# Token routing scattered in two halves, zero fills moved into a later layer, chunk rows loaded ahead of stores, and contexts loaded earlier

## The chip, the core and the metric

The program runs on one core of one Trainium2 chip. The metric is device time in microseconds (us), from the start of the program to its end. Three timed runs of the kernel before took 1674.0, 1676.03 and 1676.31 us; the median is 1676.03 us. The profile comes from one more execution. Engines are named as in the profile: PE is TensorE (PEld its weight loads), DVE is VectorE, ACT is ScalarE, POOL is GpSimd and SP is SyncE, which here only issues transfers (DMAs).

## The reference, cut to what matters

Eight sequences of 112 tokens with 256 features pass through four layers. Each layer adds a gated cross attention and a gated feed-forward part:

```python
x = x + tanh(g_xattn[2]) * L2_xattn(layernorm(x), ctx, ctx, mask_BxSxS2)   # 16 heads, 375 keys, one mask per sequence
x = x + tanh(g_ffn[2])   * L2_ffn(layernorm(x))                            # two blocks, each attention + experts
# first block of L2_ffn: _token_moe
cw  = top-2 softmax weights of h @ gate_w + gate_b           # 8 experts, 2 for each token
out = sum over e of (gelu(h @ w1[e] + b1[e]) @ w2[e] + b2[e]) * cw[..., e]
```

The other parts are computed too, but the change touches only their neighbourhood: layer 1 has 16 experts whose tokens are chosen by capacity (its rows come back through memory) and a shared expert, and layer 2's feed-forward has a second block whose experts are chosen for a whole sequence.

## The kernel before, in words

Every engine has its instruction stream written out by hand, in the order of the code; semaphores tie them together. The eight sequences are taken as two groups (`it` = 0, 1, called the first and the second group here) of four sequences (lanes, `j`). SP issues nearly all loads in one stream, and waits in that stream for the moment at which a buffer is free.

Layer 2's cross attention ("l2x") needs for each lane a context (`arena<-in_ctxT`, 375 KB) and a mask (`arena<-in_mask`, 164 KB). SP waits for the end of layer 1's shared expert (`end["sh"]`) and then issues context and mask lane by lane. For the second group each context waits for that lane's last values of the first group. PE starts a group with `keys_ahead` (lanes 0 and 1 in the second group), then transposes, then keys and queries (L581); DVE first turns the four masks into numbers (L2213).

The token experts ("tok") work on chunks of 128 rows of one expert. All 1792 token-expert pairs get a slot in a table in memory, `token_rows`. Before, the slots of an expert begin where the chunks that the experts ahead of it use end, so a slot is known only when all pairs of both groups are counted: PE counts the picks (L1851), sums them over experts (L1855), and gives the slots (L1857 to L1859); DVE makes `token_slots` of them (L2396). POOL then scatters the rows, 16 indirect DMAs (L1272), waits until they have landed, reads the number of turns into a register, and loads the rows of the first two chunks (L1280). A turn is four chunks; here there are five turns. In a turn, for each chunk PE multiplies it by the expert's first matrix (16 products of two passes), transposes the rows of the chunk after the next (L1869), and multiplies a chunk's hidden values by the second matrix. POOL waits for the transposition of a chunk's rows, which frees their buffer, loads the rows of two chunks further, and stores finished outputs (`token_outputs`, L1291). SP loads each expert's weights, 2 MB, for the next turn when PE has finished that chunk. At the end POOL gathers the outputs by the same slots (L1300).

Rows of `token_rows` that no token fills, and part of `token_outputs`, must be zero: two DMAs early in the program fill them from one block of zeros. Lines 1074 to 1078 hold these fills, 1121 to 1127 the contexts and masks, 1266 to 1292 POOL's scatter and its loop.

Of the kernel before, what the change touches and what calls it, by code (L numbers as in the profile page):

```python
# [19 lines left out]
F32 = mybir.dt.float32  # L20
BF16 = mybir.dt.bfloat16
I32 = mybir.dt.int32
# [104 lines left out]
def flamingo(nc, A, out):  # L127
    ctx = ExitStack()
    with ctx:
# [54 lines left out]
        tok_ids = sb("chunk_experts", [1, MAX_TURNS * TOK_SLOTS + 1], I32)  # L184
        hmean = sb("h_mean", [P, 2, LANES, KC])
# [145 lines left out]
        idf = arena[0:1, 3 * LB + 2400:3 * LB + 2430]  # L331
        tok_hid = [arena[:, s * LB + 2048:s * LB + 2048 + 8 * P] for s in range(2)]
# [649 lines left out]
        at["n"] = 0  # L982
        xn_all = cut(arena, B * C)[0:T, :].rearrange("t (b c) -> t b c", b=B)
        sel = cut(arena, CAP * P)[0:T, :].rearrange("t (c g) -> t c g", c=CAP)
        selw = cut(arena, CAP * P)[0:T, :].rearrange("t (g c) -> t g c", c=CAP)
        expert_rows = arena[0:T, 0:2 * B * C].rearrange("s (b h f) -> s b h f", b=B, h=2)
        xnT_all = cut(arena, KC * B * T).rearrange("p (k b t) -> p k b t", k=KC, b=B)
        taken = cut(arena, KC * E1 * B * CAP).rearrange("p (k e n) -> p k e n", k=KC, e=E1)
        selT = cut(arena, B * 2 * T)[0:T, :].rearrange("s (b h t) -> s b h t", b=B, h=2)
        eo = cut(arena, E1 * C)[0:T, :].rearrange("s (e c) -> s e c", e=E1)  # L990
        hbuf = [cut(arena, 4 * T) for _ in range(2)]
# [9 lines left out]
        tok_rows = nc.dram_tensor("token_rows", ((MAX_TURNS * TOK_SLOTS + 2) * P, C), F32, kind="Internal").ap()  # L1001
        tok_outs = nc.dram_tensor("token_outputs", (MAX_TURNS * TOK_SLOTS * P, C), F32, kind="Internal").ap()
# [32 lines left out]
        def _(sp):  # L1035
# [32 lines left out]
            for dst, name in ((w_sg, "ws_g"), (w_su, "ws_u"), (w_sd, "ws_d"), (w_gate1, "l1_gate"),  # L1068
# [42 lines left out]
            for i in range(E1 // EX_SLOTS):  # L1111
                rows_of_turn(i)

# [78 lines left out]
        def _(g):  # L1192
# [74 lines left out]
            g.wait_ge(s_route, 8)  # L1267
            g.wait_ge(*p["normed"].at(0, f_norms(0)[NORM_B2], LANES - 1))
            for b in range(B):
                for k in range(TOP2):  # L1270
                    n = b * TOP2 + k
                    g.indirect_dma_start(tok_rows, bass.IndirectOffsetOnAxis(ap=tok_slot[:, n:n + 1], axis=0),  # L1272
                                         hrow[b % LANES][:, b // LANES, :], None).then_inc(s_scat, 16)
            g.wait_ge(s_scat, 16 * PAIRS)
            g.wait_ge(s_tid, 2)
# [3 lines left out]
            def chunk_rows(it, r):  # L1279
                g.dma_start(tok_x[r % 2], tok_rows[bass.ds((it * TOK_SLOTS + r) * P, P), :]).then_inc(s_xr[r % 2], 16)  # L1280

            for r in range(2):
                chunk_rows(0, r)
# [1401 lines left out]
```

## Time and profile before

| What | Value |
|---|---|
| timed runs, median (lowest to highest) | 1676.03 us (1674.0 to 1676.31) |
| profiled execution, its own time | 1660.98 us |
| its span | 1659.6 us |
| mean granted TensorE clock | 0.97 of full speed |
| PE busy / weight loads busy | 1539.6 us (93%) / 1272.0 us (77%) |
| DVE / ACT / POOL busy | 747.2 (45%) / 680.7 (41%) / 241.7 us (15%) |
| share of PE and of DMA in the chain that ended last | 70% and 5% |
| SP's queue | 97515 packets, 143.53 MB |

The profiled execution is 15.05 us shorter than the median of the timed ones; 1.4 us of it lie outside its span. The span runs through the stages one after the other: layer 0 until about 231 us, layer 1 until 488, layer 2's cross attention until 665, the first block of its feed-forward with the token experts until 970, the second block until 1229, and layer 3 to the end. Times in the views are us from the start of the span. In a row, "idle before" in brackets is how long the engine stood idle before the instructions, and what ended that.

### The profile page before, as it was taken

How to read it: one execution, taken by the hardware profiler on the slowest of the kernel's cores; microseconds unless marked ns; L12 is line 12 of the kernel's file. 1: busy time of each engine (PE TensorE's matmuls, PEld its weight loads, DVE VectorE, ACT ScalarE, POOL GpSimd, SP SyncE). 2: the span in 40 equal slices, each digit the busy share in tenths (PEclk: the TensorE clock that was granted, in tenths of full speed). 3: DMA queues.
4: the chain of work that ended last, by engine and by line, in shares of the span. 5: the costliest groups of instructions: out<-in, count | busy, mean ns of one | idle time of the engine just before them, and what ended most of it. 6: DMA issues, size and time to landing. Idle time of an engine off the chain costs nothing.

```text
span 1659.6 us, 32141 instructions
## 1 busy us (share of the span) xinstructions
PE 1539.6 (93%) x12101; PEld 1272.0 (77%) x12101; DVE 747.2 (45%) x2634; ACT 680.7 (41%) x2151; POOL 241.7 (15%) x379
## 2 busy tenths in 40 slices
PE   7999999799989999998699978999999999999986
PEld 5787887688977777775588866878987777777865
DVE  3535565411036666864011157771124443444466
ACT  2615433322117676754233326643334443344452
POOL 2022210000001121212311133156000000000000
PEclk9999999899999999998799999889999999999999
DMA  9500011359210100401789910337930001000000
GB/s 335 204 1 1 1 42 38 115 204 292 49 54 1 55 2 2 182 2 47 238 301 310 309 36 24 103 102 239 300 109 1 1 1 38 1 1 2 1 1 23
DMA packets 103253, 156.38 MB, mean 94 GB/s; under 512 B 12231, under 2 KB 80959, under 8 KB 102535
## 3 DMA queue, kind: packets, MB, share of 16 engines
q1 hardware_dynamic: 97515, 143.53, 26.2%
q0 software_dynamic: 3552, 9.18, 1.6%
q8 instruction: 86, 1.41, 0.4%
q10 hardware_dynamic: 2048, 1.84, 0.3%
q14 instruction: 52, 0.43, 0.1%
HBM read 147.31 MB, written 11.67 MB: 96 GB/s over the span
## 4 chain that ended last, share of the span: by engine, by line
PE 70%; ACT 7%; DMA 5%; DVE 5%; issue 3%; POOL 2%; POOLq 0%; ACTq 0%; DVEq 0%
PE psum L581 43%; PE psum L678 6%; PE psum L662 5%; PE psum L702 5%; PE psum L968 5%; ACT arena L889 4%; DMA arena<-token_rows 3%; DMA expert_out<-arena 1%; PE psum L537 1%; POOL token_rows L1272 1%; PE psum L955 1%; ACT arena L903 1%; PE psum L710 1%; PE psum L547 1%; DVE arena L801 1%
## 5 line engine op out<-in xcount | busy, mean ns | idle before, releaser
L889 ACT ACTIVATE arena<-arena,rowmin 112x375 f32<-112x375 f32 (+1 forms) x584 | 292.6, 507 | 180.4 <-DVE rowmin L801 180.3
L581 PE MATMUL psum<-arena,region 128*128 128x112 f32 (+2 forms) x1920 | 325.6, 327 | 5.2 <-DMA arena<-in_ctxT 2.6
L581 PEld LDWEIGHTS psum<-arena,region 128*128 128x128 f32 x1920 | 261.9, 197 | 66.1 <-issue 5.6
L581 PE MATMUL psum<-region,arena 128*125 128x128 f32 (+4 forms) x1632 | 230.5, 291 | 9.8 <-DVE arena L790 3.7
L581 PEld LDWEIGHTS psum<-region,arena 128*125 128x125 f32 (+2 forms) x1632 | 195.5, 183 | 44.1 <-issue 18.7
L678 PEld LDWEIGHTS psum<-identity,arena 112*125 112x125 f32 (+1 forms) x1240 | 141.8, 177 | 57.9 <-ACT arena L903 17.2
L678 PE MATMUL psum<-identity,arena 112*125 112x112 f32 (+1 forms) x1240 | 165.8, 278 | 15.8 <-ACT arena L903 5.0
L581 PE MATMUL psum<-arena 128*128 128x128 f32 (+4 forms) x896 | 141.4, 315 | 0.0
L662 PE MATMUL psum<-arena 32*112 32x375 f32 (+3 forms) x912 | 133.6, 477 | 0.5 <-DVE arena L779 0.4
L581 PEld LDWEIGHTS psum<-arena 128*128 128x128 f32 (+2 forms) x896 | 125.9, 192 | 10.5 <-issue 0.3
L949 POOL COPY arena<-rinv 112x128 f32<-112x128 f32 x136 | 34.0, 293 | 581.7 <-DVE rinv L824 558.9
L889 ACT ACTIVATION_READ_ACCUMULATOR arena<-arena,rowmin 112x1 f32 x584 | 113.0, 193 | 0.0
L581 PE MATMUL psum<-arena,stream 128*128 128x128 f32 (+2 forms) x832 | 101.3, 285 | 5.7 <-ACT arena L1421 3.5
L581 PEld LDWEIGHTS psum<-arena,stream 128*128 128x128 f32 x832 | 100.2, 201 | 8.3 <-issue 6.8
L801 DVE CUSTOM_DVE_ANT_0 arena<-psum,zero_column 112x375 f32<-112x375 f32 x192 | 94.0, 545 | 18.5 <-PE psum L662 18.5
L968 PE MATMUL psum<-region,arena 128*112 128x256 f32 x432 | 96.9, 381 | 5.2 <-DVE arena L833 3.3
L1501 ACT ACTIVATE arena<-psum,moe_b 128x128 f32<-128x128 f32 x160 | 45.6, 368 | 118.5 <-PE psum L581 118.5
L968 PEld LDWEIGHTS psum<-region,arena 128*112 128x112 f32 x432 | 75.5, 177 | 23.2 <-DVE arena L833 5.2
L581 PE MATMUL psum<-stream,arena 128*112 128x256 f32 (+1 forms) x352 | 80.6, 380 | 1.9 <-DVE arena L2182 1.9
L662 PEld LDWEIGHTS psum<-arena 32*112 32x112 f32 (+2 forms) x912 | 56.7, 171 | 31.1 <-DVE rowmin L801 4.4
L492 POOL TENSOR_TENSOR x_rstd<-x_var_eps,minus_half 112x4 f32<-112x4 f32 x16 | 17.6, 1101 | 407.5 <-DVE x_var_eps L487 382.0
L801 DVE CUSTOM_DVE_ANT_0 arena<-psum,arena 112x375 f32<-112x375 f32 x136 | 67.1, 545 | 19.1 <-PE psum L662 18.7
(304 smaller groups left out, 1891.9 us busy)
## 6 DMA issues: line engine op xcount, KB each, us to landing
stream<-in_moe_w SPq DMA_DIRECT2D x36, 1024.0 KB, 7.3
arena<-in_moe_w SPq DMA_DIRECT2D x36, 1024.0 KB, 7.3
arena<-in_ctxT SPq DMA_DIRECT2D x32, 375.0 KB, 4.2
stream<-in_e_wg SPq DMA_DIRECT2D x8, 512.0 KB, 4.6
stream<-in_e_wu SPq DMA_DIRECT2D x8, 512.0 KB, 5.7
stream<-in_e_wd SPq DMA_DIRECT2D x8, 512.0 KB, 6.6
region<-in_e_wg SPq DMA_DIRECT2D x8, 512.0 KB, 7.6
region<-in_e_wu SPq DMA_DIRECT2D x8, 512.0 KB, 8.4
```

The source lines that it names most:

```text
L492: g.tensor_tensor(x_rstd[:, turn_of], x_veps[:, turn_of], minus_half[0:T, :], ALU.pow).then_inc(s_xrstd, 1)
L537: pe.matmul(to[:, 0:P], ident[:, :], ident[:, :], start=True, stop=True)
L547: last = pe.transpose(bank_t[j][:, c * T:(c + 1) * T], src[j][:, c * P:(c + 1) * P], ident[0:T, 0:T])
L581: last = pe.matmul(dst, l, r, start=(i == 0), stop=(i == n - 1))
L662: pe.matmul(bank_s[j][0:T, 0:a.group * a.keys], lhs, rhs, start=True, stop=True)\
L678: last = pe.transpose(dst[0:a.key_w, n * T:(n + 1) * T], a.masked(r, j)[0:T, i * a.key_w:(i + 1) * a.key_w], ident[0:T, 0:T])
L702: last = pe.matmul(outs[rows, j * T:(j + 1) * T], v, a.turned(r)[0:a.key_w, j, i * T:(i + 1) * T], start=(i == 0 and s % a.stay == 0), sto ...
L801: last = nc.vector.tensor_tensor_reduce(out=a.masked(r, j)[0:T, ks], in0=bank_s[j][0:T, ks], in1=a.mask(j), scale=1.0, scalar=3.0e38, op0= ...
L889: last = act.activation(e, e, ACT.Exp, bias=rowmin[:, j, n:n + 1], scale=-1.0, accum_out=rowsum[:, j, h:h + 1])
L949: last = g.tensor_copy(three(spread[j], a.heads), rinv[:, j, 0:a.heads].unsqueeze(2).broadcast_to([T, a.heads, a.d]))
L968: last = pe.matmul(to[j][0:T, 0:C], OT[j][:, c, :], w[:, c, :], start=(c == 0 and not onto), stop=(stop and c == n - 1))
L1501: last = act.activation(tok_hid[r % 2][:, m * P:(m + 1) * P], bank[r % 2 * 2 + m // 4][:, m % 4 * P:(m % 4 + 1) * P], ACT.Gelu, bias=b1q[: ...
```

## The change

Five things change.

- **Slots.** Each of the 8 experts now has room for MAX_OF = 7 chunks (`SPARE` = 56 chunks in all, and one spare chunk of zeros), so a slot depends only on the tokens ahead and not on how many chunks other experts use. The first group's slots are computed while the second group's attention output is normalised, and its 8 scatters wait only for that. A new table `chunk_rows` tells for each chunk where its rows begin; surplus chunks point at the spare one. POOL reads it into a register before each row load and each store.
- **Zero fills.** Both tables have 57 chunks now and are filled whole (before 26, and 8 of 24). The fills are taken out of the early loads; one follows the masks of the first group in l2x, the other those of the second.
- **Row loads ahead of stores.** POOL issues two more row loads before the loop, and in the loop each load comes before the store of the chunk, so a load no longer waits behind stores.
- **Contexts.** The first group's four contexts of l2x are issued right after the expert rows of layer 1. For that the expert buffers in `arena` are laid out anew.
- **Weights.** The second chunk's weights no longer wait for the scatter.

```diff
+        tok_base = sb("chunk_rows", [1, MAX_TURNS * TOK_SLOTS + 4], I32)
...
+        SPARE = E2 * MAX_OF
...
-        tok_rows = nc.dram_tensor("token_rows", ((MAX_TURNS * TOK_SLOTS + 2) * P, C), F32, kind="Internal").ap()
-        tok_outs = nc.dram_tensor("token_outputs", (MAX_TURNS * TOK_SLOTS * P, C), F32, kind="Internal").ap()
+        tok_rows = nc.dram_tensor("token_rows", ((SPARE + 1) * P, C), F32, kind="Internal").ap()
+        tok_outs = nc.dram_tensor("token_outputs", ((SPARE + 1) * P, C), F32, kind="Internal").ap()
...
-            load(tok_rows.rearrange("(c p) f -> c p f", p=P),
-                 A["zeros"].unsqueeze(0).broadcast_to([MAX_TURNS * TOK_SLOTS + 2, P, C]), s_zero)
-            n = MIN_TURNS * TOK_SLOTS
-            load(tok_outs[n * P:, :].rearrange("(c p) f -> c p f", p=P),
-                 A["zeros"].unsqueeze(0).broadcast_to([MAX_TURNS * TOK_SLOTS - n, P, C]), s_zero)
+            def clear(rows):
+                load(rows.rearrange("(c p) f -> c p f", p=P), A["zeros"].unsqueeze(0).broadcast_to([SPARE + 1, P, C]),
+                     s_zero)
...
             for i in range(E1 // EX_SLOTS):
                 rows_of_turn(i)
+            for j in range(LANES):
+                context("l2", 0, j)
...
             for it in range(ITERS):
                 for j in range(LANES):
-                    context("l2", it, j, p_l2x["v_out"].at(0, a2.tiles - 1, j) if it else None)
                     if it:
+                        context("l2", it, j, p_l2x["v_out"].at(0, a2.tiles - 1, j))
                         sp.wait_ge(*p_l2x["rowmin_ready"].at(0, a2.tiles * a2.steps - 1, j))
                     load(maskb[j].bitcast(I32), A["mask2"][it * LANES + j], s_maskl[j])
+                clear((tok_rows, tok_outs)[it])
...
             chunk_expert(0, 0)
+            chunk_expert(0, 1)
             sp.wait_ge(s_scat, 16 * PAIRS)
-            for r in range(1, TOK_SLOTS):
+            for r in range(2, TOK_SLOTS):
...
-            g.wait_ge(s_route, 8)
-            g.wait_ge(*p["normed"].at(0, f_norms(0)[NORM_B2], LANES - 1))
-            for b in range(B):
-                for k in range(TOP2):
...
+            for i in range(ITERS):
+                g.wait_ge(s_route, 5 if i == 0 else 9)
+                g.wait_ge(*p["normed"].at(0, f_norms(0)[NORM_A2 + i], LANES - 1))
+                for j in range(LANES):
+                    for k in range(TOP2):
+                        n = (i * LANES + j) * TOP2 + k
+                        g.indirect_dma_start(tok_rows, bass.IndirectOffsetOnAxis(ap=tok_slot[:, n:n + 1], axis=0),
+                                             hrow[j][:, i, :], None).then_inc(s_scat, 16)
...
+            begin = [rows_at(0, r) for r in range(2)]
+            g.wait_ge(s_scat, 16 * PAIRS)
             for r in range(2):
-                chunk_rows(0, r)
+                chunk_rows(begin[r], r)
+            for r in range(2):
+                at_ = rows_at(0, r + 2)
+                wait_first(g, *p_m[0]["tok_turned"].at(0, r))
+                chunk_rows(at_, r)
             with g.Fori(0, turns) as it:
                 for r in range(TOK_SLOTS):
-                    wait_first(g, *p["tok_turned"].at(it, r))
-                    chunk_rows(it, r + 2)
-                    for n in ([r - 1] if r else []) + ([r] if r == TOK_SLOTS - 1 else []):
...
+                    at_ = rows_at(it, r + 4)
+                    wait_first(g, *p_m[0]["tok_turned"].at(it, r + 2))
+                    chunk_rows(at_, r)
+                    keep_outputs(it, r, rows_at(it, r))
...
+            def slots_of(i, to):
+
+                of = slice(i * P // 2, (i + 1) * P // 2)
+                held_by = slice(0, (i + 1) * P // 2)
+                pe.matmul(to[0:T, 0:P // 2], before, picked[:, of], start=True, stop=False)
+                pe.matmul(to[0:T, 0:P // 2], count[held_by, :], groups_before[held_by, of], start=False, stop=False)
+                pe.matmul(to[0:T, 0:P // 2], whole_of.broadcast_to([E2, T]), chunks_before[:, of], start=False,
+                          stop=True).then_inc(s_rmm, 1)
...
+                    if l == 0 and it:
+                        pe.wait_ge(s_picks, TOP2)
+                        pe.matmul(bank[4][0:P // 2, 0:T], picked[:, 0:P // 2], one_col[0:T, 0:1].broadcast_to([T, T]),
+                                  start=True, stop=True).then_inc(s_rmm, 1)
...
+                        slots_of(0, bank[5])
...
                 norm_stats(v, p, 0, n, summed_out, lambda j: p["proj_out"].at(it, 0, j))
+                if l == 0 and it:
+                    slots_of(0, bank[5], 2, 2)
                 norm_apply(v, p, 0, n, summed_out, dst)
```

The three places where instructions move are these. First SP, from the expert rows of layer 1 to the second group's first context of l2x. Before:

```order
L1037 DMA arena<-expert_out 14x8x256 x16
L1037 DMA arena<-in_ctxT 128x2x375
L1037 DMA arena<-in_mask 112x375
L1037 DMA arena<-in_ctxT 128x2x375
L1037 DMA arena<-in_mask 112x375
L1037 DMA arena<-in_ctxT 128x2x375
```

And now:

```order
L1047 DMA arena<-expert_out 14x8x256 x16
L1047 DMA arena<-in_ctxT 128x2x375 x4
L1047 DMA arena<-in_mask 112x375 x4
L1047 DMA token_rows<-in_zeros 57x2x16384
L1047 DMA arena<-in_ctxT 128x2x375
L1047 DMA arena<-in_mask 112x375
```

The four contexts stand together ahead of the masks, and a fill of 57 x 2 runs of 16384 words (64 KB each) stands ahead of the second group's contexts in SP's queue. The fill of `token_outputs`, of the same shape, follows the second group's masks.

Next POOL, from the last norm of the first block to the first chunks' rows. Before:

```order
L522 TENSOR_SCALAR var_eps<-mean_var 112x2
L524 TENSOR_TENSOR rstd<-var_eps,minus_half 112x2
L1272 DMA token_rows<-arena,token_slots 3328x256 x16
L1276 TENSOR_LOAD chunk_experts
L1276 ISA x2
L1280 DMA arena<-token_rows 128x256 x2
```

And now:

```order
L527 TENSOR_SCALAR var_eps<-mean_var 112x2
L529 TENSOR_TENSOR rstd<-var_eps,minus_half 112x2
L1285 DMA token_rows<-arena,token_slots 7296x256 x16
L1288 TENSOR_LOAD chunk_experts
L1288 ISA x2
L1292 TENSOR_LOAD chunk_rows
L1292 ISA x2
L1292 TENSOR_LOAD chunk_rows
L1292 ISA x2
L1295 ISA
L1295 DMA arena<-token_rows 128x256
```

The 16 scatters stand where they stood (the first 8 wait for less), and two more register loads stand between them and the first row load.

Last DVE, in the second group's norm behind the attention of the first block, ahead of the gates. Before:

```order
L512 BN_STATS bn_sums<-psum 112x6 x2
L515 BN_AGGR mean_var<-bn_sums 112x2 x2
L531 TENSOR_SCALAR arena<-psum,mean_var,rstd 112x256 x4
L2230 TENSOR_TENSOR gate_small<-psum,moe_gate_bias 112x8 x4
L2234 MAX gate_small<-gate_small 112x8 x4
```

And now:

```order
L517 BN_STATS bn_sums<-psum 112x6 x2
L520 BN_AGGR mean_var<-bn_sums 112x2 x2
L2352 TENSOR_TENSOR arena<-psum,arena 112x64
L2355 TENSOR_REDUCE arena<-arena 112x8
L2357 CAST token_slots<-arena 112x8
L536 TENSOR_SCALAR arena<-psum,mean_var,rstd 112x256 x4
L2269 TENSOR_TENSOR gate_small<-psum,moe_gate_bias 112x8 x4
```

The three operations that make the first group's slots stand between the statistics and the application of the norm.

## Rows read from the trace of the kernel before

**Rows 1.** Waits of PE over the whole run: us in total, times, longest.
```profile
PE psum L1869 <- DMA arena<-token_rows: 12.2, 10, 3.8
PE psum L537 <- DMA token_rows<-arena,token_slots: 11.7, 1, 11.7
PE psum L581 <- DMA arena<-in_ctxT: 2.6, 1, 2.6
```

**Rows 2.** Timeline at the start of l2x: start, us, instruction, idle before.
```profile
487.81 0.40 SPq L1037 DMA_DIRECT2D arena<-in_ctxT  x1
...
491.39 8.73 PE L581 MATMUL psum<-arena,region 128*128 128x375 f32 x32 [2.56 <-DMA arena<-in_ctxT]
```

**Rows 3.** Timeline of PE at the start of l2x's second group.
```profile
578.35 2.69 PE L581 MATMUL psum<-arena,region 128*128 128x375 f32 x8
...
582.14 4.47 PE L581 MATMUL psum<-arena,region 128*128 128x112 f32 x24
```

**Rows 4.** Busy time by window: us, engines' busy time, PE clock, DMA share, GB/s.
```profile
490.00:495.00 5.00, 3.61 (x9) 2.49 (x10) 0.71 (x2) 0.01 (x1) 1.01 (x1) 0.66 1.07 331
```

**Rows 5.** Timeline of SP: the zero fill of token_rows.
```profile
37.89 1.07 SPq L1037 DMA_DIRECT2D token_rows<-in_zeros  x1
```

**Rows 6.** DMA view of 48.00 to 50.40; queue row: packets, MB, share of 16 engines.
```profile
DMA packets 17, 0.86 MB, mean 356 GB/s; under 512 B 1, under 2 KB 4, under 8 KB 4
...
q1 hardware_dynamic: 17, 0.86, 94.3%
```

**Rows 7.** DMA view of 53.70 to 56.50.
```profile
DMA packets 244, 0.84 MB, mean 298 GB/s; under 512 B 14, under 2 KB 154, under 8 KB 236
```

**Rows 8.** DMA view of 49.395 to 49.415, which holds one packet.
```profile
q1 hardware_dynamic: 1, 0.07, 755.6%
```

**Rows 9.** Timeline of SP: the second group's first context and last mask.
```profile
540.30 0.40 SPq L1037 DMA_DIRECT2D arena<-in_ctxT  x1
...
570.50 0.46 SPq L1037 DMA_DIRECT2D arena<-in_mask  x1
```

**Rows 10.** DMA view of 487 to 500: the first group's contexts and masks.
```profile
q1 hardware_dynamic: 1600, 2.21, 56.7%
```

**Rows 11.** Timeline from the end of attention to the first chunk.
```profile
763.81 3.62 PE L968 MATMUL psum<-region,arena 128*112 128x256 f32 x16
...
774.51 0.46 PE L1851 MATMUL psum<-one_column,arena 112*128 112x112 f32 x2 [1.93 <-DVE arena L2251]
...
779.72 0.17 DVE L2396 CAST token_slots<-arena 112x16 uint32<-112x16 f32 x1
...
780.87 1.21 POOL L1272 DMA_INDIRECT token_rows<-arena,token_slots  x1 [11.45 <-DVE token_slots L2396]
...
799.83 0.94 POOL L1272 DMA_INDIRECT token_rows<-arena,token_slots  x1 [0.30 <-issue]
802.40 3.79 PEld L537 LDWEIGHTS psum<-identity 128*128 128x128 f32 x20 [12.08 <-DMA token_rows<-arena,token_slots]
...
803.80 1.18 POOL L1280 DMA_DIRECT2D arena<-token_rows  x2 [3.03 <-issue]
...
810.20 0.69 PE L1869 MATMUL psum<-identity,arena 128*128 128x128 f32 x2 [3.82 <-DMA arena<-token_rows]
```

**Rows 12.** All that reads or writes token_rows: DMA to landing.
```profile
DMA to landing us min/median/max: 2.3/5.7/7.2
```

**Rows 13.** Timeline of the first turn's end: a row wait, and a late load.
```profile
841.13 0.44 PE L1869 MATMUL psum<-identity,arena 128*128 128x128 f32 x2 [1.91 <-DMA arena<-token_rows]
...
847.27 0.55 POOL L1280 DMA_DIRECT2D arena<-token_rows  x1 [0.56 <-issue]
```

**Rows 14.** Timeline of PE in the last turn: two chunks' second products.
```profile
954.04 3.62 PE L581 MATMUL psum<-stream,arena 128*128 128x256 f32 x16
...
961.28 3.62 PE L581 MATMUL psum<-arena 128*128 128x256 f32 x16
```

**Rows 15.** Busy time by window: the fourth turn.
```profile
909.00:940.00 31.00, 29.07 (x199) 26.91 (x198) 4.62 (x12) 10.41 (x33) 4.02 (x9) 1.00 0.91 305
```

More of the change, by code:

```diff
@@ L982, in flamingo @@
         at["n"] = 0
+        xnT_all = cut(arena, KC * B * T).rearrange("p (k b t) -> p k b t", k=KC, b=B)
+        hbuf = [arena[:, at["n"] + h * 4 * T:at["n"] + (h + 1) * 4 * T] for h in range(2)]
+        assert at["n"] + 8 * T <= off["c"]
         xn_all = cut(arena, B * C)[0:T, :].rearrange("t (b c) -> t b c", b=B)
@@ L1293, in _ @@
             for s in range(2):
-                wait_first(g, s_xr[s], turns * (8 * TOK_SLOTS) + 16)
+                wait_first(g, s_xr[s], turns * (8 * TOK_SLOTS) + 32)
                 wait_first(g, s_yst[s], turns * (8 * TOK_SLOTS))
@@ L1470, in _ @@
                     attend_scalar(act, af[l], p, it, own=(1,) if it else ((1, 2, 4, 5), (4, 5, 6))[l])
+                    if l == 0 and it:
+                        act.wait_ge(s_rmm, 1)
+                        act.copy(count[0:P // 2, :], bank[4][0:P // 2, 0:T]).then_inc(s_route, 1)
                     if l == 0:
@@ L1485, in _ @@
                     continue
-                act.wait_ge(s_rmm, 1)
+                act.wait_ge(s_rmm, 3)
                 act.copy(count, bank[0][:, 0:T]).then_inc(s_route, 1)
@@ L1852, in _ @@
                           stop=True).then_inc(s_rmm, 1)
-                pe.wait_ge(s_route, 1)
-                pe.wait_ge(s_rconst, 16 * 7)
+                pe.wait_ge(s_route, 6)
+                slots_of(1, bank[2])
                 pe.matmul(bank[1][0:E2, 0:T], of_expert, count, start=True, stop=True).then_inc(s_rmm, 1)
-                pe.wait_ge(s_route, 3)
-                pe.matmul(bank[2][0:T, 0:P], before, picked, start=True, stop=False)
-                pe.matmul(bank[2][0:T, 0:P], count, groups_before, start=False, stop=False)
-                pe.matmul(bank[2][0:T, 0:P], used.broadcast_to([E2, T]), chunks_before, start=False,
-                          stop=True).then_inc(s_rmm, 1)
-                pe.matmul(bank[3][0:T, 0:E2], used.broadcast_to([E2, T]), chunks_upto, start=True,
+                pe.wait_ge(s_route, 11)
+                pe.matmul(bank[3][0:T, 0:E2], used.broadcast_to([E2, T]), chunks_upto, start=True, stop=True)
+                pe.matmul(bank[3][0:T, E2:2 * E2], used.broadcast_to([E2, T]), ident[0:E2, 0:E2], start=True,
                           stop=True).then_inc(s_rmm, 1)
@@ L2307, in summed_out, with slots_of @@
                 return bank_s[j][0:T, 0:C]
+            def slots_of(i, src, products, done):
+                of, half = slice(i * SEQ_ITEMS, (i + 1) * SEQ_ITEMS), P // 2
+                v.wait_ge(s_rmm, products)
+                v.tensor_tensor(place[:, of, :], src[0:T, 0:half].rearrange("t (g e) -> t g e", e=E2), picks[:, of, :],
+                                ALU.mult).then_inc(s_route, 1)
+                v.wait_ge(s_route, done + 1)
+                v.tensor_reduce(placef[:, of], place[:, of, :], AX_X, ALU.add).then_inc(s_route, 1)
+                v.wait_ge(s_route, done + 2)
+                v.tensor_copy(tok_slot[:, of], placef[:, of]).then_inc(s_route, 1)
             def second_norm(p, l, it, dst):
@@ L2311, in second_norm @@
                 norm_stats(v, p, 0, n, summed_out, lambda j: p["proj_out"].at(it, 0, j))
+                if l == 0 and it:
+                    slots_of(0, bank[5], 2, 2)
                 norm_apply(v, p, 0, n, summed_out, dst)
```

64 lines of the change are left out of this document (39 added, 25 removed).

## The prediction

> **What bounds the kernel now.** I took the engines' busy time first: PE works 93% of the span, so only idle time of PE, time in which its clock is low, and new waits can move the end. Then PE's waits [rows 1]. Three of them lie where the change acts: L1869 waits 12.2 us for rows of chunks, L537 once 11.7 us for the scatter, L581 once 2.6 us for a context. Then the timelines of these places [rows 2, 3, 9, 11, 13, 14], and last the DMA views of the zero fills, because the change puts transfers that nobody waited for ahead of transfers for which PE waits [rows 5 to 8, 10]. The sum is made against the profiled execution, 1660.98 us; the median of the timed runs lies 15.05 us above it, and I take a difference in the one to be the same in the other. What this measurement can tell from no change is about 0.2%, 3.3 us.
>
> **Opening of the token experts: -9.9 us.** Before, the slots of all pairs are ready at 779.72 + 0.17 = 779.89, POOL issues its first scatter at 780.87 and the sixteenth at 799.83, so one takes (799.83 - 780.87) / 15 = 1.264 us; the last ends at 800.77. PE sees them landed at 802.40, 1.6 us later. POOL issues the row loads at 803.80, and the first transposition comes at 810.20, 6.4 us after that [rows 11]. Now 8 scatters start with the first group's slots. These come from one PE product on counts, an ACT copy, three PE products and three DVE operations, behind `project_out`, which ends at 763.81 + 3.62 = 767.43. Before's whole chain, from the count at 774.51 to the slots at 779.89, took 5.4 us and had two steps more; the last two DVE operations and the copies alone bound it below at about 1.9. I take 2.6, nearer the short end since half the columns are handled and a round trip between engines is gone: slots at 770.0, first scatter at 771.0 with the same lag of 1.0. The second group's slots, whose chain hardly changes, come at 779 to 780; POOL would want them for its ninth scatter at 771.0 + 8 x 1.264 = 781.1, so POOL never stops. Last scatter's end 771.0 + 19.9 = 790.9, landed 792.5. Of the three register loads ahead of the row loads one stood in the 1.4 us between landing and issue before; the two of rows can run while the scatters land. Rows issued at 793.9, first transposition 800.3: 9.9 us earlier. The three DVE operations delay the second group's norm by 1 to 2 us; the attention's part that PE does in the meantime ends some 6 us ahead of the rows, which hides it, and without that cover they would cost those 1 to 2. The end of the term: a chain of 5.4 us instead of 2.6 makes it -7.1; the shorter chain and rows that land in the median 5.7 us make it -11.5. Row loads took 2.3 to 7.2 us from issue to landing [rows 12], and I keep the 6.4 since both chunks' weights still stream beside them, now one of them earlier.
>
> The rows show 2.3 us for the quickest of these 128 KB loads and 5.7 for the median. The Trainium skill, "DMA: Bandwidth & Descriptors", section "Anatomy of one DMA", gives for POOL's path a fit of 2.0 us plus bytes by 436 GB/s, which is 2.3 us here. The minimum agrees, the median does not; by that rule the opening would gain some 3 us more, and I follow the rows.
>
> **The loop: -8.0 us.** Of the 12.2 us for rows the first 3.8 belong to the opening [rows 1, 11] and 0.3 lies ahead of the loop: 8.1 are left in five turns. At 847.27 POOL issues a load whose buffer was free at about 835.8, because it first waited to store outputs; PE had stood 1.91 us for the load before that one [rows 13]. Now each load stands ahead of the stores, behind only its own buffer, and two more are ahead of the loop. Where nothing waits a chunk takes 961.28 - 954.04 = 7.24 us [rows 14]; rows are then issued 10.5 to 13.8 us before their transposition, more than the longest landing of 7.2 [rows 12]. So the waits go, about 8.0. POOL has two register loads for each chunk more; before, one fitted with its issue into 1.4 us, and two of at most 1.4 are 2.8 of 7.24, beside 0.55 and 1 for the issues [rows 11, 13]. They would bind only from some 2.8 each. What could be late next is the weights: four chunks of 2.1 MB weights and 0.26 MB rows and outputs in 4 x 7.24 = 28.97 us are 326 GB/s, against 305 at a share of 0.91 in the fourth turn [rows 15]. Between 0 (weights bind at 31.1 us a turn) and -8.0 I take -8.0, since the DMA view shows 356 GB/s in the fills [rows 6] and 331 here [rows 4].
>
> **First group of l2x: -3.9 us, which the next term takes back.** The contexts are issued with layer 1's experts and the wait of 2.56 us behind them goes. The 32 first products took 8.73 us [rows 2] at a clock of 0.66 of full speed [rows 4]; in the second group the same forms took 2.69 + 4.47 = 7.16 [rows 3], since PE had not stopped. 2.5 + 1.5 is about 3.9. Nothing else is late: masks are issued as PE starts.
>
> **Zero fills: +7.8 us with that.** The removed early fills [rows 5] gain nothing, PE waits for neither. The new ones are the danger. Before, a fill of 26 blocks of 2 x 64 KB and one of 8 were made. In a window inside the first the view shows 17 packets, 4 small, so 13 of 64 KB, which fill 94.3% of 16 engines' 2.40 us [rows 6]: 13 engines, 0.943 x 16 x 2.40 / 13 = 2.79 us a packet. In a window of the second 244 packets, 236 small, so 8 large [rows 7]. 26 blocks went over 13 engines and 8 over 8: the largest number up to 16 that divides the blocks. 57 = 3 x 19, so this fill goes over 3 engines, 19 x 2 = 38 packets on each. A packet that shares little took 7.556 x 16 x 0.02 = 2.42 us [rows 8]: 38 x 2.42 = 91.9 us.
>
> The Trainium skill states that rule, in "DMA: Bandwidth & Descriptors", section "Why a DMA increments its semaphore by 16 and not by 1": the widest split up to 16 that divides the slowest dimension. The trace agrees, with 13 and 8.
>
> The first group's four masks are issued from 487.81 on [rows 2], each about 0.5 us, the fill at 489.9, data from about 491.3: it ends at 583.2. The second group's first context was issued at 540.30 and the last mask at 570.50 [rows 9]. They are in the same queue, so on 3 of 16 engines their pieces stand behind the fill. PE wants lane 0's context at 578.35 [rows 3], or 574.45 with the 3.9 gained. All four lanes' data took 0.567 x 13 = 7.4 us of the engines [rows 10], one lane 1.8, so the first context lands at 583.2 + 1.5 = 584.7. PE stands 584.7 - 574.45 = 10.2 us, ends 6.35 later than before, and starts again at the low clock, +1.5: +7.8 against before. Later lanes land 1.8 us apart, faster than PE uses them (7.16 / 4 for keys and more behind it); the masks come at about 591. The second fill then blocks the three engines from about 591 to 683. What SP issues in it is wanted from about 776 on, so it costs nothing; if the fill had its longest form below it would still be done by 710.
>
> **Sum.** 7.8 - 9.9 - 8.0 = -10.1: profiled 1650.9, median 1665.9.
>
> **Rivals.** *The fill costs more than the rest gives (0.13, slower).* Place: PE's wait for the second group's first context. A fill packet takes as long as among 13, 2.79 us and up to 2.85 with contexts beside it: 38 x 2.85 = 108.3, 16.4 more: 1682.3. It decides from 2.42 + 10.1 / 38 = 2.69 us a packet on. For it: [rows 6], packets were that slow; against: there 13 engines copied at once, here 3. *The fill spreads over all engines (0.08, faster).* 114 packets in 8 rounds of 2.8 are 22 us, done at 514, no wait and no cold start: 1665.9 - 7.8 - 3.9 = 1654.2. Against: [rows 6, 7]. *The transfers bind the loop (0.13, within 0.2%).* The 8.0 don't come, PE waits for weights in place of rows: 1673.9. For it: a share of 0.91 [rows 15]; against: no weight wait among PE's large ones [rows 1]. *The opening gains half (0.08, faster).* Register loads stand in a row behind the landing, or rows land late behind the weights issued earlier: 1670.9. Forecast: 0.58.
>
> The likeliest case's own range is 1660 to 1672: its chain 2.8, its rows 1.6, a fill packet from 2.35 to 2.5 us 3. The range over all is 1656 to 1682, which leaves out the spread fill's lower end and what is beyond the slow packets. Faster 0.58 + 0.08 + 0.08 = 0.74, within 0.2% 0.13, slower 0.13.
>
> **What would show it.** PE waits about 10 us for `in_ctxT` at 575 to 585, and the fill's windows hold 3 packets of 64 KB in about 2.4 us. No wait of 11.7 us at L537, POOL's first scatter 9.9 us ahead of before's (relative to the stage), turns of 29 us, L1869 waiting only for the first chunk. The forecast is wrong if there is no wait for `in_ctxT`, if the wait is over 20 us, or if L581 waits for weights in the turns.

## The result and the profile after

The changed kernel took 1665.82 us (median of 20 runs, 1658.93 to 1673.75), the kernel before 1675.59 us (20 runs, 1668.71 to 1678.96): ratio 0.9948, interval 0.9936 to 0.996. By the medians it is 9.8 us faster, by the interval of the ratio 6.7 to 10.7; the forecast was 10.1.

The two profiled executions do not show that: 1660.79 us against 1660.98, spans 1659.2 and 1659.6. So the profile after is read part by part here, and experiments 1 and 2 have a second profile of each kernel. First PE's waits for DMAs. Of before's three [rows 1] none is left. The one large wait now is the new one, for the second group's context:

```profile
PE psum L586 <- DMA arena<-in_ctxT: 12.5, 1, 12.5
```

PE around l2x's two groups in the changed kernel (start, us, instruction, idle before):

```profile
488.37 7.09 PE L586 MATMUL psum<-arena,region 128*128 128x375 f32 x32
...
586.37 4.62 PE L586 MATMUL psum<-arena,region 128*128 128x375 f32 x8 [12.53 <-DMA arena<-in_ctxT]
...
592.10 4.47 PE L586 MATMUL psum<-arena,region 128*128 128x112 f32 x24
```

The first group has no wait, and its 32 products take 7.09 us instead of 8.73 [rows 2]. The second group waits 12.5 us, and its first eight products take 4.62 us instead of 2.69 [rows 3]: PE had stood, and the granted clock is half from 576.4 to 590.1. SP's timeline and the DMA view of 540 to 545 show what it waited for:

```profile
489.30 0.91 SPq L1047 DMA_DIRECT2D token_rows<-in_zeros  x1
535.63 0.41 SPq L1047 DMA_DIRECT2D arena<-in_ctxT  x1
...
563.44 18.64 SPq L1047 DMA_DIRECT2D arena<-in_mask  x1
582.13 0.43 SPq L1047 DMA_DIRECT2D arena<-in_ctxT  x1
```

```profile
DMA packets 7, 0.41 MB, mean 82 GB/s; under 512 B 0, under 2 KB 0, under 8 KB 0
...
q1 hardware_dynamic: 6, 0.39, 18.1%
```

The queue moved six packets of 64 KB in 5 us, and each took 0.181 x 16 x 5 / 6 = 2.41 us. That fits 3 engines with two packets each. The second group's first context was issued at 535.63, behind the fill, and landed 50.7 us later. One mask's issue took 18.64 us and returned at 582.08, when the last packets of 64 KB ended. So the fill held back SP as well, and with it all that SP had still to issue.

The opening of the token experts, PE, POOL and ACT:

```profile
773.72 3.62 PE L973 MATMUL psum<-region,arena 128*112 128x256 f32 x16
780.85 1.21 POOL L1285 DMA_INDIRECT token_rows<-arena,token_slots  x1 [1.51 <-issue]
...
797.34 0.52 ACT L1466 COPY arena<-psum 8x448 f32<-8x448 f32 x1 [10.01 <-remote]
799.80 0.94 POOL L1285 DMA_INDIRECT token_rows<-arena,token_slots  x1 [0.31 <-issue]
805.65 1.18 POOL L1295 DMA_DIRECT2D arena<-token_rows  x2 [4.91 <-DMA token_rows<-arena,token_slots]
811.73 4.10 PE L542 MATMUL psum<-identity 128*128 128x128 f32 x20 [0.82 <-ACT arena L1471]
815.66 0.60 PE L1908 MATMUL psum<-identity,arena 128*128 128x128 f32 x4
```

From `project_out`'s end at 777.34 the first scatter is 3.5 us away, where it was 780.87 - 767.43 = 13.4 [rows 11]. But from the last scatter's end (800.74) to the row loads it is now 4.9 us instead of 3.0, and in this execution PE waits for neither the scatter nor the rows: its gate work came late behind ACT's copy, whose wait no engine of this core ends ("remote"). The loop, by window (us, engines' busy time, PE clock, DMA share, GB/s):

```profile
830.00:860.00 30.00, 30.00 (x211) 28.30 (x210) 4.52 (x12) 11.32 (x37) 4.37 (x8) 1.00 0.97 320
860.00:890.00 30.00, 30.00 (x210) 28.25 (x209) 4.69 (x13) 10.88 (x35) 4.36 (x8) 1.00 0.97 330
```

PE is busy all the time, at a share of 0.97 and 330 GB/s, where it was 29.07 of 31.00 us at 0.91 and 305 [rows 15]. Last, a stretch that the profile before does not have:

```profile
995.14 0.49 PE L542 MATMUL psum<-identity 128*128 128x128 f32 x2
996.35 0.36 PE L542 MATMUL psum<-identity 128*128 128x128 f32 x1 [0.72 <-issue]
997.75 0.40 PE L542 MATMUL psum<-identity 128*128 128x128 f32 x2 [1.05 <-issue]
999.22 0.35 PE L542 MATMUL psum<-identity 128*128 128x128 f32 x1 [1.06 <-issue]
1000.61 0.37 PE L542 MATMUL psum<-identity 128*128 128x128 f32 x1 [1.04 <-issue]
```

PE issues one product every 1.4 us. The matching products lie 6.2 us ahead of before's on one side of this stretch (995.14 and 1001.37) and 0.2 behind them on the other (1002.59 and 1002.36). This is where the gain of this profile went.

**Where each kernel's time lies.** The table takes four pieces from the timelines of all profiles. Piece l2x goes from one product near the end of layer 1 (at 480.0 in before's profile, the same product in each) to the products at 582.14 [rows 3] in l2x's second group. The opening goes from the start of `project_out` (763.81) to the first transposition (810.20), the turns from there to the last chunk's second products (961.28 in [rows 14]). The rest ends some 4.7 us before the end of the span. Two stretches are left out, since no term of the prediction lies in them: up to l2x's piece (479.2 to 485.3 us in these profiles) and between l2x and the opening (181.6 to 184.3). They differ by up to 6 us from one execution to the next, so spans alone can't be compared. Times in us.

| kernel | l2x | opening | turns | rest |
|---|---|---|---|---|
| before, two profiles | 102.1, 102.0 | 46.4, 46.9 | 151.1, 155.6 | 693.7, 693.8 |
| changed, two profiles | 112.4, 113.4 | 41.9, 38.8 | 139.1, 141.7 | 699.7, 693.6 |
| changed, 64 blocks | 97.8 | 38.8 | 141.7 | 693.5 |
| changed, 16 x 57 pieces | 97.8 | 38.9 | 141.7 | 693.5 |
| changed, fills last | 97.8 | 48.9 | 139.2 | 690.6 |
| changed, contexts late | 115.6 | 38.9 | 141.6 | 693.5 |
| changed, 58 blocks | 160.1 | 39.2 | 141.5 | 693.4 |
| before, loads ahead of stores | 101.8 | 46.7 | 141.4 | 693.2 |
| before, new fills | 116.0 | 46.6 | 152.5 | 692.2 |
| 64 blocks, weights late | 97.8 | 36.7 | 139.1 | 693.1 |
| 64 blocks, scatter late | 97.8 | 45.2 | 140.9 | 692.8 |
| 64 blocks, contexts late | 101.7 | 37.3 | 141.4 | 692.4 |

### The profile page after: what moved, and what is told of

It reads as the page before. It is cut to its first block, busy times and chain, and to the rows that moved or that the text cites. A ratio compares the mean times of both kernels' runs of the same rounds, so it can differ in the third digit from the quotient of the medians.

```text
span 1659.2 us, 32378 instructions
## 1 busy us (share of the span) xinstructions
PE 1542.5 (93%) x12111; PEld 1272.3 (77%) x12111; DVE 748.8 (45%) x2644; ACT 680.8 (41%) x2152; POOL 242.7 (15%) x382
## 4 chain that ended last, share of the span: by engine, by line
PE 74%; ACT 8%; DVE 4%; issue 3%; another core or an unknown queue 1%; DMA 1%; POOL 1%; ACTq 0%; DVEq 0%; POOLq 0%
PE psum L586 46%; PE psum L683 6%; PE psum L667 5%; PE psum L707 5%; PE psum L973 5%; ACT arena L894 4%; PE psum L542 1%; DMA expert_out<-arena 1%; PE psum L960 1%; ACT arena L908 1%; PE psum L715 1%; PE psum L552 1%; DVE arena L806 1%; PE psum L1790 1%
## 5 line engine op out<-in xcount | busy, mean ns | idle before, releaser
L586 PE MATMUL psum<-arena,region 128*128 128x112 f32 (+2 forms) x1920 | 325.4, 326 | 15.2 <-DMA arena<-in_ctxT 12.5
L586 PE MATMUL psum<-region,arena 128*125 128x128 f32 (+4 forms) x1632 | 230.8, 291 | 10.1 <-DVE arena L795 3.9
L586 PEld LDWEIGHTS psum<-arena 128*128 128x128 f32 (+2 forms) x896 | 124.1, 189 | 10.6 <-issue 0.3
```

The source lines that it names most:

```text
L586: last = pe.matmul(dst, l, r, start=(i == 0), stop=(i == n - 1))
```

## The experiments

Ratios are to the kernel before, run beside each kernel on the same chip. The runs come in three sets: experiments 1, 3, 6 and 7; 2, 5, 9 and 10; 4, 8, 11 and 12. Within a set times can be compared directly, between sets only ratios can.

**1. The changed kernel once more.** No edit.

> The changed kernel, unchanged, once more. Its first profile shows two odd stretches, which no wait explains: at 793.8 to 803.6 SP's small instructions take 0.70 us each and ACT's copy for the gates starts 5.5 us after PE has finished its input, and at 995.1 to 1002.6 PE stands 1 us between single products with the releaser 'issue' (8.2 us lost there against before). Theory A (they belong to that one execution, whatever caused them): both are absent here, PE's wait for in_ctxT is again 12 to 13 us, and the distance from the kernel before is again about -10 us (ratio 0.994). Theory B (they belong to this kernel's code or data flow): both are here again, in the same places, and the distance is the same.

Measured 1656.57 us, ratio 0.9944 (0.9923 to 0.9965). The odd stretches are absent; the same copy of ACT starts when PE has finished, and the row loads bind:

```profile
796.68 0.52 ACT L1466 COPY arena<-psum 8x448 f32<-8x448 f32 x1 [4.50 <-PE psum L1782]
```

```profile
817.43 0.69 PE L1908 MATMUL psum<-identity,arena 128*128 128x128 f32 x2 [3.10 <-DMA arena<-token_rows]
```

The opening is 38.8 us instead of 41.9, the rest 693.6 instead of 699.7. That is theory A: they belonged to one execution. What made them stays open. In the first profile the longer opening was in part paid back: its turns take 139.1 us, here 141.7, because there PE had not stood just before them.

**2. The kernel before once more.** No edit.

> The kernel before, unchanged, once more, for a second profile. Its first profile took 1660.98 us against a median of 1675.6. Theory (PE's low-clock stretches differ from execution to execution): ratio 1.000 within its interval, the profile longer than the first by some us, with the same waits (12 us for rows, 12 for the scatter, 3 for the first context) and more time at half clock. Rival (the first profile left a wait out): a wait of PE that the first one does not have.

Ratio 0.9994 (0.9973 to 1.0016). The profiled span is 1666.3 us, 6.7 longer than the first, and 4.5 of these lie in the turns. That the waits would stay the same did not come true: those for rows rose from 12.2 to 14.2 us, and one of them was followed by half clock (907.8 to 911.3):

```profile
PE psum L1869 <- DMA arena<-token_rows: 14.2, 10, 3.3
```

```profile
907.10 0.44 PE L1869 MATMUL psum<-identity,arena 128*128 128x128 f32 x2 [2.00 <-DMA arena<-token_rows]
907.38 5.31 PE L581 MATMUL psum<-arena 128*128 128x256 f32 x16
```

Sixteen products take 5.31 us there and 3.62 elsewhere [rows 14]. The same loop took 151.1 us in the first profile, 155.6 in this one and 152.5 in experiment 9, so the first profile was the luckiest of three in its turns.

**3. 64 blocks in the fills.**

```
+        FILLED = 64
...
-        tok_rows = nc.dram_tensor("token_rows", ((SPARE + 1) * P, C), F32, kind="Internal").ap()
+        tok_rows = nc.dram_tensor("token_rows", (FILLED * P, C), F32, kind="Internal").ap()
```

and the same for `token_outputs` and for the number of blocks in `clear`.

> The changed kernel with 64 instead of 57 blocks in both tables (the fills write 64 x 2 runs of 64 KB; the seven further blocks are never read). Theory of the prediction (a fill is spread over the largest number of engines up to 16 that divides its blocks): 16 engines, 8 packets of about 2.8 us each, the fill ends about 22 us after its start, at 514; PE's wait for in_ctxT of 12.5 us is gone, as is the restart at the low clock, and the time is some 14 us below the changed kernel: ratio to before about 0.986. Rival (the volume of the fills is what delays the contexts, so 12% more of it delays them more): the wait is 14 us or more and the time 1 to 2 us above the changed kernel, ratio 0.995 to 0.996.

Measured 1641.21 us, ratio 0.9844 (0.9819 to 0.9868); the changed kernel in the same set took 1656.57. So a fill of 12% more bytes makes the kernel 15.4 us faster. PE waits for no context; the l2x piece is 97.8 us instead of 112.4 and 113.4. In the DMA view of 500 to 520 the fill now uses all the engines:

```profile
DMA packets 99, 6.44 MB, mean 322 GB/s; under 512 B 0, under 2 KB 0, under 8 KB 0
...
q1 hardware_dynamic: 98, 6.42, 101.3%
```

These are 98 packets of 64 KB at a full share of 16 engines: 1.013 x 16 x 20 / 98 = 3.3 us each. A packet takes longer than the 2.41 us that it took beside two others, but 16 are under way at a time.

**4. 58 blocks.** The same edit with 58.

> The changed kernel with 58 instead of 57 blocks in both tables (one more, never read). Theory (the largest number up to 16 that divides the blocks sets the engines): 58 = 2 x 29, so 2 engines with 58 packets of 2.42 us each: the fill takes 140.4 us instead of 92, PE's wait for in_ctxT is 12.6 + 48.4 = 61 us, and the time is 48 us above the changed kernel: ratio to before 1.023. Rival (the fill's time follows its volume): 1.6 us more, ratio 0.995 to 0.996.

Measured 1705.0 us, ratio 1.0241 (1.0205 to 1.0277). One block more costs about 48 us: the l2x piece is 160.1 us instead of 112.4 and 113.4. The wait, and the DMA view of 540 to 545:

```profile
PE psum L587 <- DMA arena<-in_ctxT: 60.1, 1, 60.1
```

```profile
q1 hardware_dynamic: 4, 0.26, 12.1%
```

Four packets in 5 us at 0.121 x 16 x 5 / 4 = 2.42 us each fit 2 engines. The rule that the prediction took from 26 and 8 blocks, the largest number up to 16 that divides the blocks, holds for 57, 58 and 64.

**5. 57 blocks in pieces of 8 KB, 16 outermost.**

```
-                load(rows.rearrange("(c p) f -> c p f", p=P), A["zeros"].unsqueeze(0).broadcast_to([SPARE + 1, P, C]),
+                load(rows.rearrange("(c q r) f -> q c (r f)", q=16, r=8),
+                     A["zeros"].rearrange("(q r) f -> q (r f)", q=16).unsqueeze(1).broadcast_to([16, SPARE + 1, 8 * C]),
```

> The changed kernel with its 57 blocks filled by 16 x 57 pieces of 8 KB, the 16 outermost, in place of 57 x 2 of 64 KB. Theory (the outermost number sets the engines, the volume their time): 16 engines, 57 packets each, the fill takes about as long as the one of 64 blocks (27 us) less a tenth, no wait for in_ctxT, ratio about 0.984 as with 64 blocks. Rival (small pieces are slower, or the division by 57 is what counts): a fill of over 60 us, or a wait for the context.

Measured 1645.19 us, ratio 0.9865 (0.9834 to 0.9897), not told apart from 64 blocks; the profiles agree in each piece of the table within 0.1 us. With 57 blocks, and with pieces of 8 KB, PE waits for no context: it is the outermost number that counts.

**6. Both fills behind the second group's masks.**

```
-                clear((tok_rows, tok_outs)[it])
+            clear(tok_rows)
+            clear(tok_outs)
```

> The changed kernel with both fills behind the second group's masks of l2x (they stay 57 blocks). Theory of the prediction (only the place in SP's queue ahead of the contexts hurts): the wait for in_ctxT is gone, both fills run on 3 engines from about 567 to 751, before POOL's first scatter at about 766, and nothing waits: about 14 us below the changed kernel, ratio about 0.986, as with 64 blocks. Rival (a fill on 3 engines delays whatever is loaded beside it): PE waits for layer 2's feed-forward or routing constants, or POOL waits for the zeros at its first scatter; then it lies 5 to 14 us above the version with 64 blocks.

Measured 1652.9 us, ratio 0.9914 (0.9887 to 0.994), 11.7 us above 64 blocks. The context's wait is gone, another has its place:

```profile
PE psum L1839 <- DMA arena<-in_of_expert: 10.7, 1, 10.7
```

The rival was right. SP's timeline shows how the fills reach this constant:

```profile
669.11 61.79 SPq L1047 DMA_DIRECT2D region<-in_l_wv  x1
730.94 27.70 SPq L1047 DMA_DIRECT2D region<-in_l_wo  x1
...
776.07 0.37 SPq L1047 DMA_DIRECT2D arena<-in_of_expert  x1
```

Two issues of weights behind the fills took SP 61.79 and 27.70 us, where they took 0.50 and 0.60 with 64 blocks. So `in_of_expert` was issued only at 776.07 (684.76 with 64 blocks), 6.5 us after PE had come to it, when the fills had been over for some 17 us. The fills cost time here by holding the engine that issues, not by standing ahead of this constant on the same 3 DMA engines. The bad shape costs wherever something wanted stands behind it in SP's stream; moving it only chose another victim. The profiled spans differ by 5.9 us, the medians by 11.7; the rest of the difference is not in the profile.

**7. The first group's contexts as before.**

```
-            for j in range(LANES):
-                context("l2", 0, j)
...
+                    context("l2", it, j, p_l2x["v_out"].at(0, a2.tiles - 1, j) if it else None)
```

> The changed kernel with the first group's four contexts of l2x issued where they were before, each ahead of its mask. Theory of the prediction (the early contexts gain 4 us at the start of l2x, and PE's wait behind the fill takes them back, since the fill starts at the same time): PE waits 2.6 us at the start, the first group ends 4.4 us later, the wait for the second group's context is shorter by as much (8 us), and the time equals the changed kernel's within 1 us, ratio 0.994. Rival (the gain at the start stays): the time is 4 us above the changed kernel, ratio 0.9965.

Measured 1662.47 us, ratio 0.9972 (0.9953 to 0.999): above the changed kernel (0.9944), where no difference was expected; the intervals overlap. The profile has 115.6 us against 113.4 for l2x, and a wait of 11.4 us, not 8. Half of the theory fell: the contexts are in the same queue ahead of the fill, so late contexts also start the fill later. It is issued at 497.02, 11.9 us into the l2x piece, instead of 492.11, which is 9.6 into it. The early contexts' gain is taken back only in part: the l2x piece keeps 2.2 of 3.9 us.

**8. The same on 64 blocks.** The edit of 7 in the kernel of 3.

> The version with 64 blocks, with the first group's contexts issued as before, each ahead of its mask. Theory (with no fill ahead of the second group's contexts nothing takes the gain back): the first group ends 4.2 us later and nothing else changes, ratio to before 0.987. Rival (early contexts are hidden by something else): no difference to the version with 64 blocks, 0.9844.

Measured 1647.63 us, ratio 0.9904 (0.9875 to 0.9933). The l2x piece is 101.7 us instead of 97.8, 3.9 us, as the term had it. The ratios differ by more, 0.6% or 10 us, and their intervals do not overlap (the upper end of 64 blocks is 0.9868). That more is not in the profile, whose span is even 0.6 us shorter than that of 64 blocks, and the two were measured in different sets. So the 3.9 us rest on the profile alone, and the other 6 stay unexplained.

**9. Before, with new fills alone.** The early fills are taken out of the kernel before, and

```
+                clear((tok_rows, tok_outs)[it])
```

stands behind each group's masks, with 57 blocks.

> The kernel before with its early fills taken out and fills of 57 blocks put behind the first and the second group's masks of l2x, nothing else. Prediction's mechanism, with the first contexts not early: the fill's data start some 4.5 us later than in the changed kernel, it runs 92 to 93 us on 3 engines, PE waits about 11 to 12 us for the second group's context and restarts at the low clock: +13 us, ratio 1.008. Rival (the early fills cost something at the start, which comes back here, or the stall needs the early contexts): +5 us or less, ratio below 1.003.

Measured 1678.73 us, ratio 1.0086 (1.005 to 1.0122), 14.4 us slower. l2x takes 116.0 us instead of 102.0; PE waits 12.3 us for the second group's context. The fills' price is there without any of the rest. Taking out the early fills shows no gain at the start: the stretch up to the l2x piece takes 479.2 us here, 480.0 and 480.3 in the kernel before, and 479.7 to 485.3 in the kernels with the change, which lack the early fills too.

**10. Before, with row loads ahead of stores.**

```
+            for r in range(2):
+                wait_first(g, *p_m[0]["tok_turned"].at(0, r))
+                chunk_rows(0, r + 2)
...
-                    wait_first(g, *p["tok_turned"].at(it, r))
-                    chunk_rows(it, r + 2)
-                    for n in ([r - 1] if r else []) + ([r] if r == TOK_SLOTS - 1 else []):
...
+                for n in range(TOK_SLOTS):
+                    wait_first(g, *p["tok_turned"].at(it, n + 2))
+                    chunk_rows(it, n + 4)
...
```

The store of chunk n follows its load. The early fill has 28 blocks instead of 26, since two more chunks are loaded.

> The kernel before with POOL's loop alone changed: each row load stands ahead of the store of its chunk and two more stand ahead of the loop (28 instead of 26 blocks in the early fill); chunks keep their places, so there are no further register loads. Prediction's term: -8.0, waits of L1869 inside the loop gone. The changed kernel's loop measured 9.7 us less. So ratio 0.994 to 0.995, and turns of 29.0 us instead of 31.1. Rival (in the changed kernel something else made the loop faster, such as the weights loaded earlier): less than half of it, ratio above 0.9975, with PE waiting for weights.

Measured 1653.55 us, ratio 0.9907 (0.9875 to 0.9938). The turns take 141.4 us, as in the changed kernel, against 151.1 to 155.6, and no wait for rows is left in them. PE in a window of this kernel:

```profile
830.00:860.00 30.00, 30.00 (x212) 28.30 (x211) 4.52 (x12) 10.94 (x36) 4.37 (x8) 1.00 0.95 322
```

This one edit of POOL's order gains at least as much as the whole change (0.9948 and 0.9944), and it owes nothing to the weights or the scatter.

**11. 64 blocks, scatters all behind the second group's slots.**

```
+            g.wait_ge(s_route, 9)
+            g.wait_ge(*p["normed"].at(0, f_norms(0)[NORM_B2], LANES - 1))
             for i in range(ITERS):
-                g.wait_ge(s_route, 5 if i == 0 else 9)
-                g.wait_ge(*p["normed"].at(0, f_norms(0)[NORM_A2 + i], LANES - 1))
```

> The version with 64 blocks, with all 16 scatters behind the second group's slots, as in the kernel before; the slots are still computed group by group. There the first scatter is at 771.6 and the second group's slots are ready at 780.4. Theory of the prediction: the first scatter starts at 781.4, 9.8 us later, and all of it comes through to the first transposition, 9 to 10 us more, ratio to before 0.990. Rival (the opening is bound by weights and row loads, not by POOL's scatter): 4 us or less, ratio 0.987 or lower.

Measured 1648.89 us, ratio 0.9912 (0.9879 to 0.9945). The opening is 45.2 us instead of 38.8: 6.4 us, between theory and rival. POOL at the scatter's end, here and then in the kernel with 64 blocks:

```profile
798.46 0.94 POOL L1286 DMA_INDIRECT token_rows<-arena,token_slots  x1 [0.30 <-issue]
802.30 1.18 POOL L1296 DMA_DIRECT2D arena<-token_rows  x2 [2.89 <-DMA token_rows<-arena,token_slots]
```

```profile
790.56 0.94 POOL L1286 DMA_INDIRECT token_rows<-arena,token_slots  x1 [0.30 <-issue]
796.82 1.18 POOL L1296 DMA_DIRECT2D arena<-token_rows  x2 [5.32 <-DMA token_rows<-arena,token_slots]
```

After the end of the late scatter the row loads come in 2.9 us: the DMA engines' share is 0.19 from 799 to 803, so the weights have mostly passed. After the early one they come in 5.3 us, beside the weights of two chunks, at a share of 1.06 to 1.07 from 792 to 800. So of the 9.8 us by which the scatter is earlier 2.4 go there, 1.0 goes into slower row loads, and 6.4 come through.

**12. 64 blocks, second chunk's weights behind the scatter.**

```
-            chunk_expert(0, 1)
             sp.wait_ge(s_scat, 16 * PAIRS)
-            for r in range(2, TOK_SLOTS):
+            for r in range(1, TOK_SLOTS):
```

> The version with 64 blocks, and the second chunk's weights of the first turn again behind the end of the scatter, as in the kernel before. In the version with 64 blocks the last scatter ends at 791.5 and POOL sees the rows landed at 796.06, 4.6 us later, while 4 MB of weights stream; before it was 1.6 to 2.6. Theory (the second chunk's weights slow the landing): landing is 2 to 3 us earlier and PE's first transposition 2 us earlier, the second chunk's weights come in time as they did before, ratio to before 0.983, 1 to 2 us below the version with 64 blocks. Rival (the weights are needed early): PE waits for in_moe_w or the rows of later chunks, and it is 1 to 4 us slower than the version with 64 blocks.

POOL and PE in this kernel:

```profile
794.11 1.18 POOL L1295 DMA_DIRECT2D arena<-token_rows  x2 [3.68 <-DMA token_rows<-arena,token_slots]
```

```profile
796.11 4.10 PE L543 MATMUL psum<-identity 128*128 128x128 f32 x20 [0.82 <-ACT arena L1471]
800.05 0.38 PE L1908 MATMUL psum<-identity,arena 128*128 128x128 f32 x2
800.80 0.44 PE L1908 MATMUL psum<-identity,arena 128*128 128x128 f32 x2 [0.37 <-DMA arena<-token_rows]
801.25 7.41 PE L587 MATMUL psum<-arena,stream 128*128 128x128 f32 x64
```

The row loads come 1.6 us sooner after the scatter (3.68 us instead of 5.32), and the opening is 36.7 us instead of 38.8. The rows arrive as PE's filling products end. So PE hardly stands (0.37 us instead of 3.1), and its first 64 products take 7.41 us instead of 9.69: the turns are shorter by another 2.6. No PE wait names weights. By its profile this is the best version, 4.7 us below 64 blocks in the two pieces. Timed: 1640.27 us, ratio 0.9855 (0.9822 to 0.9888), while 64 blocks had 0.9844 (0.9819 to 0.9868) in another set, so the two are not told apart by time, and the gain is shown by the profile alone. Both lie about 15 us below the changed kernel.

## Why the prediction was right, step by step

**Fills.** The mechanism was right: 3 engines, packets of 2.41 us, a fill that ends at about 582 (forecast 583.2), and PE waiting for the second group's context. Its size was low. The l2x piece was to grow from 102.1 to 109.9 us, by 7.8; it grew by 10.3 and 11.4 in the two profiles. PE stood 12.5 us instead of 10.2: it came at 586.37 - 12.53 = 573.84 instead of 574.45, and the context was there at 586.37 instead of 584.7. The restart at half clock cost 4.62 - 2.69 = 1.9 us instead of 1.5, and 5.37 - 2.69 = 2.7 in the second profile. That the fill also holds SP was not foreseen; here it cost nothing, in experiment 6 it was the whole cost.

**Contexts.** The forecast was -3.9, and the profile of experiment 8 has 3.9. That the fill takes all of it back was wrong in its reasoning (experiment 7). There is one queue, and what stands ahead of the fill sets when the fill starts.

**Opening.** The forecast was -9.9, measured are -7.6 to -8.1 in the undisturbed profile. The chain of 2.6 us was right to 0.1 (slots 779.87 - 777.34 = 2.53), and POOL never stopped between the groups. The landing was the step that failed: from the last scatter's end to the row loads the prediction kept before's 3.0 us, and it is 4.9 to 5.4 with two chunks' weights in the queues. From the row loads to the transposition it is 803.23 - 796.82 = 6.4 us with 64 blocks, as forecast. The edit "second chunk's weights earlier", to which the prediction gave no price, costs the 2 us and some clock: with it undone the opening is 36.7 us, 9.7 below before's 46.4 (experiment 12).

**Turns.** The forecast was -8.0, measured are -9.4 (151.1 to 141.7) to -16.5 (155.6 to 139.1). That every wait for rows goes was right, and the transfers did not bind: 330 GB/s were had where 326 were wanted. The term was mis-sized: 8.1 us of waits were one execution's, another had 10.2. And a wait can be dearer than its length: behind one of them 16 products took 5.31 us instead of 3.62, at half clock.

**Sum.** +10.3 to +11.4, -4.5 to -8.1, -9.4 to -16.5 by whichever pair of profiles one takes; the two second profiles alone give 11.4 - 8.1 - 13.9 = -10.6. The median fell by 9.8. The forecast of 10.1 hit it with a stall 2.5 to 3.6 too small, an opening about 2 too large (5 in the disturbed execution) and turns too cautious by 1.4 or more. So the total is right to half a microsecond by luck: three terms mis-sized by 1.4 to 3.6 us or more cancelled. The signs of the terms were right for the reasons given.

**Rivals.** The slow fill packets did not come: they took 2.41 us. The fill used all 16 engines only with another outermost number (experiments 3 and 5). That the transfers bind the loop is refuted by PE's 30.00 busy us of 30.00. The opening that gains half (4.5 us) was seen in one execution only, behind a stretch that no wait explains; but its second reason, rows that land late behind the weights issued earlier, is what took 1.9 and 2.4 us in the two profiles of the changed kernel.

## What to carry to other kernels

Ask of every large transfer on how many DMA engines its outermost number lets it run, and what stands behind it in its queue, and what its issuer still has to issue: 57, 58 and 64 blocks of one fill took the l2x piece to 112, 160 and 98 us. Issue loads for which an engine waits ahead of stores for which nobody does. And when the profiled execution lies at the edge of the timed runs, size terms from a second profile as well.

## What the runs showed of the hardware

- Transfers behind a slow one can hold the engine that issues them: one mask's issue took 18.64 us on SP, usually 0.46, and with both fills in a row two issues took 61.79 and 27.70. The last of these ended with the fill each time. How much the queue takes before that no run shows.
- A packet of 64 KB from memory to memory took 2.41 us with 3 engines copying, 2.42 with 2 and 3.3 with 16.
- In the first of two profiled executions of the changed kernel PE issued a product only every 1.4 us for 7 us, and ACT started 5.5 us after its input was ready; no wait of this core explains either. The Trainium skill, "NOTIFIC — the notification-queue block", section "7.1 Overflow: three behaviours, one of which stalls the engine", describes one way in which recording can hold an engine. No run here shows whether that happened.
- Executions of one kernel differ by more than this change makes: 20 runs of the changed kernel range over 14.8 us, and the longer ones have the lower mean clock, from 0.969 (1658.93 us) to 0.958 (1673.75 us).
